# Masked first layer: mask loaded earlier, block 0 added in token halves, first-column products placed ahead of the last weight sums

## Time and profile before

| | us |
|---|---|
| median of 3 runs | 498.71 |
| lowest, highest | 498.37, 498.96 |
| profiled execution, its time | 499.24 |
| its span, first to last instruction | 497.4 |
| TensorE busy | 491.2 (99%) |
| VectorE busy | 340.1 (68%) |
| ScalarE busy | 258.5 (52%) |
| GpSimd busy | 13.2 (3%) |

### The profile page before, as it was taken

One profiled execution on the slowest core, in us unless ns is written; L12 is line 12 of the kernel. 1 busy time (PEld: TensorE's weight loads), 2 busy tenths in 40 slices (PEclk: granted clock), 3 DMA queues, 4 the chain that ended last, 5 costly groups with the idle time before them and its releaser, 6 DMA issues.

```text
span 497.4 us, 6505 instructions
## 1 busy us (share of the span) xinstructions
PE 491.2 (99%) x2178; PEld 402.6 (81%) x2178; DVE 340.1 (68%) x589; ACT 258.5 (52%) x406; POOL 13.2 (3%) x18
## 2 busy tenths in 40 slices
PE   7999999999999999999999999999999999999997
PEld 3778888888888888888888888888888888888886
DVE  3767886877778676766766766566575666655655
ACT  4575563566656353555664445455554555444441
POOL 1710000000000000000000000000000000000000
PEclk9999999999999999999999999999999999999999
DMA  8955322232333243233333332232333232231002
GB/s 312 412 222 168 95 73 87 95 96 96 98 97 95 93 138 95 65 100 95 97 104 101 103 113 97 69 98 88 116 103 91 77 123 96 95 96 32 1 1 84
DMA packets 21200, 53.68 MB, mean 108 GB/s; under 512 B 2864, under 2 KB 3888, under 8 KB 20912
## 3 DMA queue, kind: packets, MB, share of 16 engines
q1 hardware_dynamic: 20304, 51.70, 31.9%
q10 hardware_dynamic: 864, 1.57, 0.8%
HBM read 51.17 MB, written 2.10 MB: 107 GB/s over the span
## 4 chain that ended last, share of the span: by engine, by line
PE 95%; DMA 1%; DVE 1%; ACT 1%; issue 1%; SPq 0%; DVEq 0%; ACTq 0%
PE act_ps L312 10%; PE act_ps L304 10%; PE act_ps L308 10%; PE acc_ps L304 10%; PE acc_ps L308 10%; PE lin_ps L312 10%; PE lin_ps L304 10%; PE acc_ps L312 10%; PE lin_ps L308 10%; DMA mask<-mask_in 1%; PE aux_ps L312 1%; PE aux_ps L308 1%; PE aux_ps L304 1%; DVE hid L808 1%; PE act_ps L351 1%
## 5 line engine op out<-in xcount | busy, mean ns | idle before, releaser
L806 DVE TENSOR_TENSOR hid<-lin_ps,act 128x512 f32<-128x512 f32 x96 | 66.4, 691 | 100.5 <-PE lin_ps L312 100.5
L797 DVE TENSOR_TENSOR w_lo<-raw,w_hi 128x384 fp32r<-128x384 f32 (+1 forms) x217 | 120.5, 555 | 0.0
L554 ACT ACTIVATE act<-act_ps 128x512 f32<-128x512 f32 x96 | 57.4, 598 | 120.4 <-PE act_ps L312 120.4
L560 ACT ACTIVATE hid_hi<-hid 128x512 fp32r<-128x512 f32 x112 | 70.8, 632 | 86.0 <-DVE hid L806 71.5
L814 DVE TENSOR_TENSOR hid_lo<-hid,hid_hi 128x512 fp32r<-128x512 f32 x112 | 77.4, 691 | 25.8 <-ACT hid_hi L560 25.8
L542 ACT ACTIVATE w_hi<-raw 128x768 fp32r<-128x768 f32 x110 | 92.2, 838 | 0.3 <-DMA raw<-w_in 0.3
L304 PE MATMUL acc_ps<-hid_hi,w_hi 128*128 128x512 f32 x224 | 87.3, 390 | 0.1
L312 PE MATMUL acc_ps<-hid_lo,w_hi 128*128 128x512 f32 x224 | 87.2, 389 | 0.0
L308 PE MATMUL acc_ps<-hid_hi,w_lo 128*128 128x512 f32 x224 | 87.2, 389 | 0.0
L304 PE MATMUL act_ps<-x_hi,w_hi 128*128 128x512 f32 x224 | 69.0, 389 | 0.0
L312 PE MATMUL act_ps<-x_lo,w_hi 128*128 128x512 f32 x224 | 69.0, 389 | 0.0
(11 more groups left out here) (114 smaller groups left out, 326.7 us busy)
## 6 DMA issues: line engine op xcount, KB each, us to landing
raw<-w_in SPq DMA_DIRECT2D x110, 384.0 KB, 3.0
cols_w<-w_in SPq DMA_DIRECT2D x2, 1024.0 KB, 9.9
out<-x SPq DMA_DIRECT2D x7, 256.0 KB, 3.6
x<-x_in SPq DMA_DIRECT2D x3, 512.0 KB, 5.9
cols_w<-w0r_in ACTq DMA_DIRECT2D x5, 256.0 KB, 5.2
cols_w<-w0r_in SPq DMA_DIRECT2D x2, 256.0 KB, 4.5
raw<-w_in SPq DMA_DIRECT2D x2, 256.0 KB, 4.6
cols_w<-w0r_in SPq DMA_DIRECT2D x1, 288.0 KB, 4.0
```

What stands on the lines that cost most here:

```text
L554: act_e.activation(act[:, n % 2, :], act_ps[:, n % 2, :], func, bias=bias).then_inc(act_ready, 1)
L560: act_e.activation(hid_hi[:, n % 2, :], hid[:, n % 2, :], ACT.Copy).then_inc(hid_hi_ready, 1)
L797: ins = dve.tensor_tensor(w_lo[:, n % SPLIT, a:z], raw[:, n % RAW, a:z], w_hi[:, n % SPLIT, a:z].bitcast(F32), ALU.subtract)
L806: ins = dve.tensor_tensor(hid[:, n % 2, :], lin_ps[:, n % 2, :], act[:, n % 2, :], ALU.mult)
```

## The change: loads, orders and halves

Row 0 of x gets a tensor of its own, `x0`, loaded by SP in two transfers. Mask 0 goes from SP to ACT, second there; w0r 3 becomes ACT's third transfer; w0r 5 and 6 are issued later. Layer 0's block 0 is computed and added in two halves of 256 tokens (the second half in a free bank). The second low part of row 0's x is made by GpSimd, between the two short and the two long subtractions; VectorE's part of that split stands behind the additions. On TensorE three products (pairs) of column block 0 stand ahead of `sum_row0(1, 1)` and two between it and `layer0_row0_split`; one stands behind it. The split of tile 4's weights moves into tile 3, behind its activation and its `hidden`.

```diff
+        x0 = sb("x0", [P, CB, T])
...
+        def l0_row0_half(half):
+
+            return aux_ps[:, 0, 0:T // 2] if half == 0 else acc_ps[:, 0, T // 2:T]
...
             load_w0r(sp, 0)
             load_w0r(sp, 2)
-            sp.dma_start(x_part(x_flat, 0, 0), x_d[0, :, 0:T]).then_inc(x0_in[0], 16)
-            load_mask(0)
+            for c in range(CB):
+                sp.dma_start(x0[:, c, :], x_d[0, :, c * T:(c + 1) * T]).then_inc(x0_in[c], 16)
...
                 pe.wait_ge(w0_masked_ready, 1)
-                for c in range(CB):
-                    pe.wait_ge(x0_in[c], 16)
-                    ins = pe.matmul(aux_ps[:, 0, :], w0_masked[:, c * P:(c + 1) * P], x_part(x_flat, 0, c),
-                                    start=c == 0, stop=c == CB - 1)
-                ins.then_inc(l0_done, 1)
+                for half in range(2):
+                    for c in range(CB):
+                        if half == 0:
+                            pe.wait_ge(x0_in[c], 16)
+                        ins = pe.matmul(l0_row0_half(half), w0_masked[:, c * P:(c + 1) * P],
+                                        x0[:, c, half * T // 2:(half + 1) * T // 2], start=c == 0, stop=c == CB - 1)
+                    ins.then_inc((l0_half_done, l0_done)[half], 1)
...
+                pe.wait_ge(x_lo_ready[0], 1)
+                pe.wait_ge(x0_lo_last, 1)
                 for c in range(CB):
-                    pe.wait_ge(x_lo_ready[0], c + 1)
                     pe.matmul(out, wh[c], x_part(x0_lo, 0, c), start=False, stop=False)
...
             first_tile(0, 0, "lh")
+            first_tile(1, 0, "hh")
             sum_row0(1, 1)
-            first_tile(1, 0, "hh")
             first_tile(1, 0, "lh")
+            first_tile(0, 0, "hl")
             layer0_row0_split()
-            first_tile(0, 0, "hl")
-            first_tile(1, 0, "hl")
             first_tile(0, 1, "hh")
             first_tile(0, 1, "lh")
-            first_tile(1, 1, "hh")
+            first_tile(1, 0, "hl")
             first_tile(0, 1, "hl")
-            first_tile(1, 1, "lh")
-            first_tile(1, 1, "hl")
+            for kind in ("hh", "lh", "hl"):
+                first_tile(1, 1, kind)
...
             load_w0r(act_e, 1)
+            load_mask(act_e, 0)
             load_w0r(act_e, 3)
-            act_e.dma_start(x_part(x_flat, 0, 1), x_d[0, :, T:2 * T]).then_inc(x0_in[1], 16)
             load_w0r(act_e, 4)
-            load_w0r(act_e, 5)
...
             selectors()
-            load_w0r(act_e, 6)
+            load_w0r(act_e, 5)
...
             act_e.activation(r_exp[:, :, :], r_low[:, :, :], ACT.Exp).then_inc(route_exp, 1)
+            load_w0r(act_e, 6)
...
+                if n == TILES1 - 1:
+                    split_weights(n + 1)
...
-                if n == TILES1 - 2:
-                    split_weights(n + AHEAD)
...
+            def add_l0_row0_block0():
+
+                dve.wait_ge(l0_half_done, 1)
+                add_l0_row0_half(0, x_part(x_hi, 0, 0), x1_half_hi)
+                dve.wait_ge(l0_done, 1)
+                add_l0_row0_half(1, x_part(x_hi, 0, 0), x_hi_ready[1])
+                add_l0_row0_half(0, x_part(x_flat, 0, 0), l0_half_added)
+                add_l0_row0_half(1, x_part(x_flat, 0, 0), l0_added)
...
             mask_row0_whole()
-            split_x0(0, 0)
-            split_x0(0, 1)
-            add_l0_row0(0)
+            add_l0_row0_block0()
+            split_x0_row0()
             mask_row0_split()
-            add_l0_row0(1)
+            add_l0_row0_block1()
...
+                if n == TILES1 - 1:
+                    split_weights(n + 1, 0)
...
-                if n == TILES1 - 2:
-                    split_weights(ahead, 0, 1)
+                if n == TILES1 - 1:
+                    split_weights(n + 1, 1)
...
+            split_first(0, 0)
+            split_first(1, 0)
+            pool.wait_ge(x_hi_ready[0], 2)
+            pool.tensor_tensor(x_part(x0_lo, 0, 1), x0[:, 1, :], x_part(x0_hi, 0, 1).bitcast(F32),
+                               ALU.subtract).then_inc(x0_lo_last, 1)
+            split_first(0, 1)
+            split_first(1, 1)
```

More of the change, by code:

```diff
@@ L158, in build @@
         l0_added = sem("l0_added")
+        l0_half_done = sem("l0_half_done")
+        l0_half_added = sem("l0_half_added")
+        x1_half_hi = sem("x1_half_hi")
+        x0_lo_last = sem("x0_lo_last")
         x_hi_ready = [sem(f"x_hi_ready{layer}") for layer in range(4)]
@@ L225, in build, with load_mask @@
             (B - 1, CB - 1, 0, T // 2), (B - 1, CB - 1, T // 2, T // 2)]
+        def load_mask(queue, m):
+            queue.dma_start(w0_half(mask[:, :], m), mask_d[:, m * D:(m + 1) * D]).then_inc(mask_in[m], 16)
         def load_w0r(queue, q):
@@ L246, in store, with load_fore @@
                     sp.dma_start(out_d[b, :, m, t:t + count], x[:, b, m, t:t + count]).then_inc(out_stored, 16)
-            def load_mask(m):
-                sp.dma_start(w0_half(mask[:, :], m), mask_d[:, m * D:(m + 1) * D]).then_inc(mask_in[m], 16)
             load_w0r(sp, 0)
             load_w0r(sp, 2)
-            sp.dma_start(x_part(x_flat, 0, 0), x_d[0, :, 0:T]).then_inc(x0_in[0], 16)
-            load_mask(0)
+            for c in range(CB):
+                sp.dma_start(x0[:, c, :], x_d[0, :, c * T:(c + 1) * T]).then_inc(x0_in[c], 16)
             sp.wait_ge(expert_ready, 1)
             e = sp.value_load(expert[0:1, 0, 0:1], min_val=0, max_val=E - 1)
-            for n in range(2):
+            def load_fore(n):
                 sp.dma_start(raw[:, n, 0:FORE],
                              w1_d[bass.ds(e, 1), n, :, 0:FORE].rearrange("a p n -> (a p) n")).then_inc(fore_in[n], 16)
-            load_mask(1)
+            load_fore(0)
+            load_fore(1)
+            load_mask(sp, 1)
             load_w0r(sp, 7)
@@ L320, in wait_lo @@
                 def wait_lo(c):
-                    pe.wait_ge(x_lo_ready[layer], b * CB + c + 1)
+                    pe.wait_ge(x_lo_ready[layer], b * CB + c + (0 if layer == 0 else 1))
                 return wait_hi, wait_lo
@@ L575, in split_x0 @@
                         act_e.wait_ge(x0_in[c], 16)
-                    act_e.activation(x_part(x0_hi, b % 2, c), x_part(x_flat, b, c), ACT.Copy).then_inc(x_hi_ready[0], 1)
+                    act_e.activation(x_part(x0_hi, b % 2, c), x0[:, c, :] if b == 0 else x_part(x_flat, b, c),
+                                     ACT.Copy).then_inc(x_hi_ready[0], 1)
             def split_x(layer, b, c):
@@ L783, in split_x0 @@
             def split_x0(b, c):
+                if (b, c) == (1, 0):
+                    dve.wait_ge(x0_lo_last, 1)
                 dve.wait_ge(x_hi_ready[0], b * CB + c + 1)
@@ L786, in split_x0, with split_x0_row0 @@
                                   x_part(x0_hi, b % 2, c).bitcast(F32), ALU.subtract).then_inc(x_lo_ready[0], 1)
+            def split_x0_row0():
+                dve.wait_ge(x_hi_ready[0], 1)
+                dve.tensor_tensor(x_part(x0_lo, 0, 0), x0[:, 0, :], x_part(x0_hi, 0, 0).bitcast(F32),
+                                  ALU.subtract).then_inc(x_lo_ready[0], 1)
             def split_x(layer, b, c):
@@ L821, in add_l0, with add_l0_row0_half, add_l0_row0_block1 @@
                                          op0=ALU.add, op1=ALU.add).then_inc(l0_added, 1)
[L823 to L827, removed]
+            def add_l0_row0_half(half, out, done):
+                t, z = half * T // 2, (half + 1) * T // 2
+                dve.scalar_tensor_tensor(out=out[:, t:z], in0=l0_row0_half(half), scalar=cols[:, C_B0:C_B0 + 1],
+                                         in1=x0[:, 0, t:z], op0=ALU.add, op1=ALU.add).then_inc(done, 1)
+            def add_l0_row0_block0():
[5 more added lines that the diff above has]
+                add_l0_row0_half(1, x_part(x_flat, 0, 0), l0_added)
+                dve.wait_ge(x1_half_hi, 1)
+                dve.wait_ge(l0_half_added, 1)
+                dve.wait_ge(l0_added, 1)
+                split_x(1, 0, 0)
+            def add_l0_row0_block1():
+                dve.wait_ge(l0_done, 2)
+                bias = cols[:, C_B0 + 1:C_B0 + 2]
+                dve.scalar_tensor_tensor(out=x_part(x_hi, 0, 1), in0=aux_ps[:, 1, :], scalar=bias, in1=x0[:, 1, :],
                                          op0=ALU.add, op1=ALU.add).then_inc(x_hi_ready[1], 1)
-                dve.wait_ge(x_hi_ready[0], c + 1)
-                dve.scalar_tensor_tensor(out=x[:, 0, c, :], in0=aux_ps[:, c, :], scalar=bias, in1=x[:, 0, c, :],
+                dve.scalar_tensor_tensor(out=x[:, 0, 1, :], in0=aux_ps[:, 1, :], scalar=bias, in1=x0[:, 1, :],
                                          op0=ALU.add, op1=ALU.add).then_inc(l0_added, 1)
-                dve.wait_ge(l0_added, c + 1)
-                split_x(1, 0, c)
+                dve.wait_ge(l0_added, 2)
+                split_x(1, 0, 1)
             def add_block(k):
@@ L991, in _, with split_first @@
```

(7 more changed lines are left out.)

## The result

| | before | changed |
|---|---|---|
| median of 12 runs, us | 498.60 | 499.75 |
| lowest, highest | 498.26, 499.08 | 498.73, 500.12 |
| profiled execution, its span | 499.24, 497.4 | 499.45, 497.6 |

A forecast was written before the change was run, and what follows sets the result against it. TensorE was taken as the bound, without slack from 40 to 490 us, so the first 32 us decide. Head 0.84 - 0.7, port wait +0.2 and tile 4's split -0.40 gave -0.06: 498.6 us, range 497.9 to 499.5.

The forecast's parts named there:

- Start of layer 0: Head of the kernel: the mask lands earlier, w0r piece 3 lands at 7.4, and TensorE starts layer 0 at 8.5 us.
- G: Gain at the end of layer 0's first matmuls, 10.5 instead of 11.18: 0.7 us, bounds 0.2 and 1.15.
- The port: SBUF access where VectorE and GpSimd instructions exclude one another; a wait was expected at `w0_lo`, between GpSimd's two long subtractions.
- L: Time that a late `w0_lo` takes from TensorE: 0.2 us, bounds 0 and 0.6.
- The 0.88 us row: Profile row of the kernel before: `w0_lo` (128x256) took 0.88 us with a GpSimd subtraction running, some 0.45 of it waiting.
- The rival: Slower case: `w0_lo`, between GpSimd's long subtractions, ends after 16.1; 499.3 us, chance 0.22, of which 0.06 beyond 0.2%.
- The moved products: At block 1 nothing covers the wait for `x_hi`; its first product ends at 17.94, first tiles at 20.97 instead of 20.83.
- Tile 4's split: At layer 1's last tile, moving the split lets `hid_lo` end near 30.0 instead of 31.14; TensorE's 0.40 us wait goes.
- Token halves: Layer 0's block 0: 0.42 us half additions make `x_hi` whole at 10.96; `sum_row0(1, 0)` covers them until 11.5, no gain or cost.
- The sum again: Whole forecast: 0.84 - G + L - 0.40 = -0.06 us, bounds -0.7 and +0.85.
- The 0.84: Delay of the first tiles' end in the new product order, before G is subtracted: 0.84 us.

The follow-up runs named there:

- the first pair of profiles: First profiled executions of the kernel before (499.24 us) and of the changed kernel (499.45 us), neither edited further.
- the lower group: Faster executions of the unedited changed kernel: seven of 11 times when measured again, from 498.63 to 499.15 us.
- the upper group: Slower executions of the unedited changed kernel: four of 11, 500.00 to 500.49 us; profiled only with tile 4's split put back to its old place (500.05).
- the second pair: Second profiled executions, both kernels unedited: the kernel before 498.35 us, the changed kernel 498.95 us.
- the second run: The changed kernel measured again with no edit: 498.98 us (11 runs), ratio 1.0015 to the kernel before.

## Why the prediction missed, step by step

- **Start of layer 0: the step that failed.** I let G = 0.7, with 0.2 as its bound. Measured: 0.18 in the first pair of profiles, 0.04 in the second. Over all profiles layer 0 starts at 8.68 on average where the mask is the gate (five: 9.19, 8.41, 8.66, 8.60, 8.55) and at 8.63 where piece 3 is (seven, from 8.37 to 9.01): the two gates tie, and G is about 0.05. My 8.5 for the changed kernel was near; the 9.19 of before that I set against it was late. Piece 3 landed at 7.74, 7.09 and 7.14 in three profiles of the changed kernel (I took 7.4), and the mask of before at 8.69 and 7.91. I compared an estimate for a usual execution with one profile, whose load happened to be late by 0.8. The sign stood in the prediction: the profile lay 0.53 above the median, and I still took a gain measured against the profile off the median. I also left 0.6 us from piece 3 to VectorE's start, where 0.79 passed: the half sum takes 0.65, not 0.5, behind an idle TensorE.
- **The port: right as a mechanism, too small, and at another place.** I took L = 0.2, with 0.6 as the bound. In the lower group it is about 0.1 (the pair at L438 takes 0.51 to 0.59 instead of 0.46). In the upper group TensorE stands 0.69 us for `w_hi` alone, and the head is 0.9 longer. I had looked for the wait at `w0_lo`; it lies on the two `x_lo` subtractions ahead of it, which the change moved onto GpSimd's busiest stretch. The 0.88 us row had shown the mechanism. The rule of the Trainium skill that I had set beside it (SBUF — State Buffer, "Who interferes with whom") is borne out by these subtractions: whoever issues first keeps the other out, to within 0.03 us of start. Beside GpSimd's TENSOR_SCALAR instructions (0.92 us alone) the rows are less clear: in the first profile of the changed kernel VectorE issued a subtraction at 18.59, within one that ran from 18.35 to 19.27, and it took 0.77 us, only 0.08 more than alone, while GpSimd's next took 1.70. The rival's price, 499.3, lay nearer to the result than my forecast, but the rival had the wait at another place and the wrong start of layer 0.
- **The moved products: right.** TensorE idles 0.84 us ahead of `first_tile(0, 1, "hh")`, whose first product ends at 18.45, where I had 17.94; the 0.5 is what the start came late. Undoing the order is worth 0.9 to 1.1 us.
- **Tile 4's split: right for the kernel before (0.45), wrong as a term of this sum.** With the new product order the hole goes by itself. The kernel did lose the hole, so the sum stood, but by a cause that I had not named; that was luck.
- **Token halves: the rows fit**, with 0.48 a piece instead of 0.42: `x_hi` was ready at 11.5 in the first profile, `sum_row0(1, 0)` ended at 12.0. No run takes the halves back.
- **The sum again.** The 0.84 was reckoned from a profile of before that lost 0.16 us at L422; the second lost 0.03, so for the second pair it is 0.97. Then 0.97 - 0.04 + 0.13 - 0.48 = +0.58 for the lower group, where 0.57 was found at `up(4)`; the upper group adds about 0.9, and its later start 0.3. A mixture of both can give the ratio's 0.95 us. What share of the executions falls in the upper group isn't settled: it was 4 of 11 in the second run, while the first 12 times spread evenly over 498.7 to 500.1, perhaps since late loads (0.6 us) and lost races blur into one another there.

## What to carry to other kernels

A single profile is one execution: before a gain is made of a load's landing, its scatter has to be known, and here it was 0.8 us, as much as the whole gain. When two engines share a resource that one holds for an instruction, work handed from the one to the other isn't free even if both have time; put it where the other issues nothing, or make it wait. And products that cover a wait are needed there: move them ahead of the work that the wait is for, and the wait lies open.

## What the runs showed of the hardware

- VectorE's 128x512 subtraction with both inputs in SBUF: 0.68 to 0.69 us alone, 1.48 to 1.78 with GpSimd's subtraction issued ahead. GpSimd's: 1.27 to 1.30 undisturbed, 1.73 to 1.80 if VectorE came first, by 0.03 to 0.22 us.
- VectorE's additions that read PSUM and one SBUF tensor ran beside GpSimd's at their usual 0.48 and 0.75 us.
- GpSimd's TENSOR_SCALAR of 128x256: 0.92 us alone, 1.70 in three profiles of the changed kernel beside VectorE's 128x768 subtraction, which took its usual 0.95.
- The same transfer, issued at the same 2.12 us, landed at 7.91 and at 8.69 in two executions of one kernel.
- Four matmuls of a sum took 0.65 us behind an idle TensorE, where eight in a full stream took 0.99.
